# A four-layer vision tower on one core: zero matmuls in TensorE's waits, norms by ACT's root, and a rebuilt last layer

## The reference

```
h = patches @ W.T + b
layer 0: gated attention (relu(q k / 1024 + bias)^2, u * (kernel @ v) @ Wo); 8 experts of 256 hidden, top 1, capacity, relu
layer 1: complex linear recurrence over the 36 tokens of an image;           8 experts of 64 hidden, top 2, gelu
layer 2: scores = max over d of (Q + K), causal, top 8 of 36, softmax, @ V;  8 experts of 128 hidden, top 2, gelu, own norm inside
layer 3: attention softmax(h W h.T / 8) h;                                   H = gelu(h W1 + b1), 256 wide; 8 experts, top 1:
         out = probs[e] * (H @ Wd[e] + bd[e])
```

## Time and profile before

| what | us |
|---|---|
| median of 3 runs (225.05 to 229.84) | 228.05 |
| the profiled execution | 227.43 |
| its span, first to last instruction | 225.6 |
| busy in it: PE, DVE, ACT, POOL | 154.4, 106.0, 54.9, 35.2 |
| mean granted TensorE clock | 0.71 of 2.4 GHz |

### The profile page before, as it was taken

How to read it: one execution, slowest core, us unless ns; L and a number is a source line. 1 busy time by engine, 2 the same in 40 slices (tenths; PEclk the granted TensorE clock), 3 DMA queues, 4 the chain that set the end, 5 groups by cost and what they waited for, 6 DMA issues and landing times.

```text
span 225.6 us, 2568 instructions
## 1 busy us (share of the span) xinstructions
PE 154.4 (68%) x972; PEld 86.0 (38%) x972; DVE 106.0 (47%) x318; ACT 54.9 (24%) x89; POOL 35.2 (16%) x79
## 2 busy tenths in 40 slices
PE   0977289789996467896829301659996836999820
PEld 0435174544432324533513001446533425684220
DVE  2013762445566172652658996127372131024952
ACT  5302900155560000250100004204530250500100
POOL 7125000227760202002000000040002002000010
PEclk9995855589999555587666955575898575556975
DMA  6999100000000000000220000000000000000001
GB/s 194 407 292 375 64 3 0 0 3 1 1 0 3 0 0 0 0 1 0 32 49 1 0 0 0 3 0 0 3 0 1 0 3 0 0 0 0 0 0 26
DMA packets 4908, 8.25 MB, mean 37 GB/s; under 512 B 2744, under 2 KB 2872, under 8 KB 4768
## 3 DMA queue, kind: packets, MB, share of 16 engines
q1 hardware_dynamic: 4896, 8.10, 11.1%
HBM read 7.73 MB, written 0.37 MB: 36 GB/s over the span
## 4 chain that ended last, share of the span: by engine, by line
PE 50%; DVE 20%; issue 15%; POOL 5%; ACT 4%; DMA 4%; POOLq 1%; DVEq 0%
PE ps L400 11%; PE ps L413 7%; POOL rstd L284 5%; PE ps L371 4%; PE ps L364 3%; PE ps L407 3%; PE ps L465 3%; DVE scores L1090 3%; PE ps L382 2%; DVE hidden_gated L926 2%; PE ps L502 2%; DVE scores_rest L1101 2%; DMA weights_sb<-weights 1%; DMA k_parts_img<-k_scratch 1%; ACT squares L715 1%
## 5 line engine op out<-in xcount | busy, mean ns | idle before, releaser
L284 POOL TENSOR_TENSOR rstd<-var_eps,minus_half 96x6 f32<-96x6 f32 (+1 forms) x8 | 11.6, 1446 | 125.1 <-DVE var_eps L869 125.1
L926 DVE TENSOR_TENSOR hidden_gated<-hidden,ps 128x288 f32<-128x288 f32 x56 | 22.2, 449 | 13.3 <-PE ps L407 13.2
L727 ACT ACTIVATE hidden<-ps,weights_sb 128x576 f32<-128x576 f32 x28 | 20.6, 740 | 31.0 <-PE ps L400 30.9
L413 PE MATMUL ps<-hidden_gated,weights_sb 128*64 128x288 f32 x112 | 19.8, 432 | 0.6 <-DVE hidden_gated L926 0.5
L371 PE MATMUL ps<-consts_sb,rstd 96*64 96x96 f32 x108 | 10.8, 376 | 12.6 <-POOL rstd L284 12.6
L400 PE MATMUL ps<-h,weights_sb 64*128 64x288 f32 x80 | 18.1, 547 | 1.6 <-DVE h L874 1.3
L864 DVE COPY centred<-ps 128x288 f32<-128x288 f32 x8 | 3.7, 457 | 26.5 <-ACT squares L715 26.5
L715 ACT ACTIVATE squares<-ps 128x288 f32<-128x288 f32 x8 | 3.3, 410 | 44.9 <-PE ps L544 13.1
L371 PEld LDWEIGHTS ps<-consts_sb,rstd 96*64 96x64 f32 x108 | 8.4, 223 | 13.3 <-POOL rstd L284 13.3
L687 PE MATMUL ps<-weights_sb,hidden 128*128 128x512 f32 (+1 forms) x20 | 12.0, 766 | 0.0
L400 PEld LDWEIGHTS ps<-h,weights_sb 64*128 64x128 f32 x80 | 8.6, 235 | 9.1 <-ACT hidden L727 4.2
(11 more groups left out here) (247 smaller groups left out, 241.6 us busy)
## 6 DMA issues: line engine op xcount, KB each, us to landing
patch_sb<-patches SPq DMA_DIRECT2D x6, 288.0 KB, 5.7
weights_sb<-weights SPq DMA_DIRECT2D x1, 1108.0 KB, 9.7
weights_sb<-weights SPq DMA_DIRECT2D x1, 749.0 KB, 15.7
weights_sb<-weights SPq DMA_DIRECT2D x1, 689.0 KB, 14.3
weights_sb<-weights SPq DMA_DIRECT2D x1, 640.0 KB, 12.9
weights_sb<-weights SPq DMA_DIRECT2D x1, 512.0 KB, 11.4
weights_sb<-weights SPq DMA_DIRECT2D x1, 394.0 KB, 13.5
weights_sb<-weights SPq DMA_DIRECT2D x1, 375.5 KB, 6.8
```

What stands on the lines that cost most here:

```text
L284: pool.tensor_tensor(RS[:, 0:n], VE[:, 0:n], mhalf[0:TT, 0:n], ALU.pow).then_inc(S["rs"], 1)
L413: last = mm(PS[rows(h), YB, 0:HALF], w2[:, ch, :], HG[:, ch % GRING, h, :], start=False, stop=(ch == chunks - 1), skip_group_check=True)
L727: act.activation(HR[:, at % RING, :, :], two(ZA if ch % 2 == 0 else ZB), func, bias=w(f"b1_{n}")[:, ch:ch + 1]).then_inc(S["act_out"], 1)
L926: dve.tensor_tensor(HG[:, at % GRING, h, :], HR[:, at % RING, h, :], PS[:, G + h, 0:HALF], ALU.mult)\
```

## The change

- **Zeros.** `idle(n, bank)` issues n matmuls of 128x512 bf16 on an operand of zeros into a bank that is free then. 153 of them stand ahead of PE's waits: six at the start; two before each variance; one or three before and two after each spread; and in the attentions, the recurrence, the guard, the softmax and layer 3's attention (groups of 1 to 10). DVE clears the operand first, and five other tiles and one of ones, 5312 elements per partition, before anything else; selectors, gates and bias rows get 128 rows instead of 48 or 1 with zeros below. The two bias matmuls of V go ahead of the patches.
- **Norms.** After its squares ACT takes the root of the variances (`Sqrt` from PSUM), DVE the reciprocal; POOL's power is gone. `table(Sqrt)` is added before each squares but one, and the table of the next function follows the root: 16 calls of `table` instead of 8.
- **Experts.** Layer 0: the gates of a pair of chunks once for both, two downs, two ups. All layers: one DVE product of 576 columns per chunk. In layers 1 and 2 the gates of later chunks go to ZA and ZB too (`GATE_AT`).
- **Attention 0.** Residual and bias row go ahead of the scores and the kernel; half of the centring of the later weights moves behind the context's product. The load of those weights goes ahead of that of layer 0's experts.
- **Attention 2.** K is made from the centred rows before the norm is spread and scaled by the root's reciprocal on DVE. POOL subtracts the maximum and scales by the sum, taken from the eight top values, beside DVE's replacements; one DVE pass then selects. The router of layer 2 takes its logits from the centred rows with weights times gamma; its bias is made ahead.
- **Layer 3's experts.** The last router's logits come transposed: `Wg` as the 8-column stationary operand, then two matmuls to turn them. The bias is added by a bf16 matmul in three parts. Weights and bias are centred, so the last norm needs no mean; ACT squares with a sum, roots, and scales four of five tiles; stores go out tile by tile.

```diff

...
-            sp.dma_start(SL[:, :], sels).then_inc(S["sels"], 16)
+            sp.wait_ge(S["rows_zero"], 3)
+            sp.dma_start(SL[0:6 * E, :], sels).then_inc(S["sels"], 16)
...
+            sp.wait_ge(S["zero3"], 3)
+            sp.dma_start(BR[0:65:32, :], bias3).then_inc(S["bias3"], 16)
...
-                pool.wait_ge(S["ve"], k + 1)
-                n = 4 * NT if k == 5 else 2 * NT
-                pool.tensor_tensor(RS[:, 0:n], VE[:, 0:n], mhalf[0:TT, 0:n], ALU.pow).then_inc(S["rs"], 1)
...
+            pool.wait_ge(S["w_r2"], 16)
+            pool.tensor_scalar(WRG[:, :], w("Wr"), w("gam2"), None, ALU.mult).then_inc(S["wr_gam"], 1)
+            cut = ((0, 3), (3, QT))
+            pool.wait_ge(S["topped"], QT * HEADS)
+            for a, b in cut:
+                pool.tensor_tensor(SE[:, a:b, :, :].rearrange("p j h s -> p (j h) s"),
+                                   SC[:, a:b, :, :].rearrange("p j h s -> p (j h) s"),
+                                   top[:, a:b, :, 0].rearrange("p j h -> p (j h)").unsqueeze(2)
+                                   .to_broadcast([P, (b - a) * HEADS, SPAD]), ALU.subtract).then_inc(S["sub2"], 1)
+            pool.wait_ge(S["top_sum"], 1)
+            for n, (a, b) in enumerate(cut):
+                pool.wait_ge(S["exp2_out"], n + 1)
+                pool.tensor_tensor(SE[:, a:b, :, :].rearrange("p j h s -> p (j h) s"),
+                                   SE[:, a:b, :, :].rearrange("p j h s -> p (j h) s"),
+                                   d20[1][:, a * HEADS:b * HEADS].unsqueeze(2).to_broadcast([P, (b - a) * HEADS, SPAD]),
+                                   ALU.mult).then_inc(S["norm2"], 1)
...
+            def idle(n, bank):
+                for _ in range(n):
+                    mm(PS[:, bank, :], idle_in[:, 0:P], idle_in[:, :], start=True, stop=True)
...

+                bank = MB if k == 4 else ZA
...
                 pe.wait_ge(S["rs"], k + 1)
                 broadcast(psBC, 0)
+                idle(2, bank)

...
-                            .then_inc(S["gates"], 1)
+                        last = mm(PS[:, bank + h, 0:HALF], sel[:, g, h, :], CT3[:, :], start=True, stop=True)
+                    last.then_inc(S["gates"], 1)

...
+                    for pair in range(E):
+                        gate(pair, G, 2 * pair - 1 if pair > 0 else None)
+                        if pair == 0:
+                            bias2(True)
+                        else:
+                            down(2 * pair - 2)
+                            down(2 * pair - 1)
+                        for ch in (2 * pair + 6, 2 * pair + 7):
+                            if ch < chunks:
+                                up(ch)
+                    down(chunks - 2)
+                    down(chunks - 1)
...
+                        down(ch)
+                else:
+                    gate(0, G)
+                    up(7)
+                    gate(1, G, 0)
+                    pe.wait_ge(S["act_out"], BASE[2] + 7)
+                    gate(2, ZA)
+                    bias2(True)
+                    pe.wait_ge(S["act_out"], BASE[2] + 8)
+                    gate(3, ZB)
+                    gate(4, G, 1)
+                    down(0)
...
+            pe.wait_ge(S["filled"], 3)
+            pe.wait_ge(S["tok_w"], 16)
+            for j in range(2):
+                mm(PS[:, ZB + j, :].rearrange("p (a e) -> p a e", a=4), ones[:, 0:P],
+                   w("bv_row").unsqueeze(1).to_broadcast([P, 4, P]), start=True, stop=False, skip_group_check=True)
             pe.wait_ge(S["rows_c"], 2)
...
+            idle(8, G)
             pe.wait_ge(S["q_ready"], 1)
+            idle(4, G)
...
+            pe.wait_ge(S["wo_c"], 1)
+            mm(psY, w("bo_row"), ones[:, :], start=False, stop=False, skip_group_check=True)
+            idle(2, G)
...
+            for t in range(NT):
+                last = mm(PS[0:TT, ZA, t * P:(t + 1) * P], XC[:, cols(t)], w("wk"), start=True, stop=True)
+            last.then_inc(S["k_done"], 1)
...
+            idle(8, ZA + 1)
+            pe.wait_ge(S["wr_bet"], 1)
             pe.wait_ge(S["q_parts"], 3)
+            idle(10, MB)
...
                     n += 1
+            pe.wait_ge(S["score_red"], n)
+            idle(7, MB)
+            pe.wait_ge(S["topped"], QT * HEADS)
+            idle(7, MB)
+            pe.wait_ge(S["top_sum"], 1)
+            idle(7, MB)
+            pe.wait_ge(S["replaced"], QT * HEADS)
+            idle(4, MB)
...
+            pe.wait_ge(S["wr_gam"], 1)
+            pe.wait_ge(S["xc"], 6)
+            logits(2, XC, WRG[:, :])
+            idle(1, ZA)
             pe.wait_ge(S["rs"], 6)
...
+                return HH[:, ch, 4 * P:TOK] if q == 0 else HH[:, ch, (q - 1) * P:q * P]
+            def y3(q):
...
+                mm(PS[32 * h:32 * h + 32, YB, 0:D], HP[:, 2 * P:HALF], c("ident")[:, rows(h)], start=True, stop=True)
+            for q in range(1, FT):
+                last = mm(PS[:, YB, q * D:(q + 1) * D], HP[:, ((q - 1) % 2) * P:((q - 1) % 2 + 1) * P],
+                          c("ident")[:, rows((q - 1) // 2)], start=True, stop=True)
...
+            def bias(q):
+                mm(y3(q), one3[:, 0:n3(q)], BD3[:, :], start=True, stop=False, skip_group_check=True)
+            def part(q, ch):
...
+            def logits_T(ch):
+                for q in range(1, FT):
+                    mm(PS[32 * (q - 1):32 * (q - 1) + E, MB, 0:P], w("Wg")[:, ch * E:(ch + 1) * E], tok3(q, ch),
+                       start=False, stop=(ch == 1), skip_group_check=True)
+                return mm(PS[0:E, MB, P:P + 64], w("Wg")[:, ch * E:(ch + 1) * E], tok3(0, ch),
+                          start=False, stop=(ch == 1), skip_group_check=True)
...
-                for ch in range(2):
-                    last = mm(PS[0:n3(i), MB, i * E:(i + 1) * E], tok3(i, ch), w("Wg")[:, ch * E:(ch + 1) * E],
-                              start=(ch == 0), stop=(ch == 1))
...
+            part(0, 0)
+            pe.wait_ge(S["logits3_in"], 1)
...
+            for q in range(1, FT):
+                bias(q)
+                part(q, 0)
+                part(q, 1).then_inc(S["y3_done"], 1)
...
+                act.wait_ge(S["var"], k + 1)
+                if k == 5:
+                    act.activation(SD[0:TT, 2 * NT:4 * NT], psVar, ACT.Sqrt, bias=eps[0:TT, 1:2], scale=1.0 + EPS)\
+                       .then_inc(S["sd"], 1)
+                act.activation(SD[0:TT, 0:2 * NT], psVar, ACT.Sqrt, bias=eps[0:TT, 0:1]).then_inc(S["sd"], 1)
...
+                act.wait_ge(S["tile3"], q + 1)
+                act.activation(R2[0:p, q, :], R[0:p, q, :], ACT.Square, accum_out=ss[0:p, q:q + 1]).then_inc(S["ss"], 1)
...
-                if k == 5:
-                    step(dve.tensor_scalar(VE[:, 2 * NT:4 * NT], psVar, 1.0 + EPS, EPS * EPS, ALU.mult, ALU.add))
-                    sync()
-                dve.tensor_scalar(VE[:, 0:2 * NT], psVar, EPS, None, ALU.add).then_inc(S["ve"], 1)
...
+            dve.memset(idle_in[:, :], 0.0).then_inc(S["still"], 1)
+            dve.memset(SL[:, :], 0.0).then_inc(S["rows_zero"], 1)
+            dve.memset(CT3[:, :], 0.0).then_inc(S["rows_zero"], 1)
+            dve.memset(CTF[:, :], 0.0).then_inc(S["rows_zero"], 1)
+            dve.memset(BD3[:, :], 0.0).then_inc(S["zero3"], 1)
+            dve.memset(one3[:, :], 1.0).then_inc(S["zero3"], 1)
+            dve.memset(BR[:, :], 0.0).then_inc(S["zero3"], 1)
...
                 return x.rearrange("p (h t e) -> p h t e", h=2, t=NT)

-            dve.tensor_copy(by_half(kp3[:, 0, :]), psK).then_inc(S["k_parts"], 1)
...
+            te20 = TE[:, :, :, :].rearrange("p j h s -> p (j h) s")
...
+                    link(dve.tensor_reduce(d20[0][:, :], te20, AX, ALU.add))
+                    dve.reciprocal(d20[1][:, :], d20[0][:, :]).then_inc(S["top_sum"], 1)
                 for h in range(HEADS):
-                    step(dve.match_replace(REP[:, j, h, :], top[:, j, h, :], SC[:, j, h, :], 3 * NEG))
...
+                        .then_inc(S["replaced"], 1)
+            dve.wait_ge(S["replaced"], QT * HEADS)
+            dve.wait_ge(S["norm2"], 2)
+            dve.scalar_tensor_tensor(PR[:, :, :, 0:SPAD].rearrange("p j h s -> p (j h) s"),
...
+                dve.wait_ge(S["y3_done"], q + 1)
+                step(dve.tensor_tensor(YM[0:p, q, :, 0:E],
+                                       PS[0:p, 4 if q == 0 else q - 1, :].rearrange("p (d e) -> p d e", e=E),
+                                       comb[0:p, q, :].unsqueeze(1).to_broadcast([p, D, E]), ALU.mult))
...
+                dve.wait_ge(S["hres_in"], 1 if q == 0 else 2)
+                sync()
+                dve.tensor_reduce(R[0:p, q, :], YM[0:p, q, :, :], AX, ALU.add).then_inc(S["tile3"], 1)
```

449 lines of the change are left out of this document (262 added, 187 removed).

## The result

The changed kernel takes **169.44 us** (median of 4, 169.17 to 169.58) against 226.91 (4 runs, 225.05 to 229.84) of the kernel before on the same chip: ratio 0.749, 95% interval 0.744 to 0.754. The forecast was 179.5 with a range from 167 to 198, so the kernel gained 57.5 us where 47.8 were forecast (from 227.43, the profiled execution). Its profiled execution took 169.38, with a span of 167.5.

What follows compares the result with a forecast made beforehand. The kernel was taken as one dependent chain, bound by link lengths and TensorE's low clock. Ten stage savings sum to 58.7 us; less 3, 5 and 2.9, 47.8 off 227.43 gives 179.6, stated as 179.5, range 167 to 198.

Steps and rivals of the forecast that it cites:

- the deduction of 10.9: Whole kernel: allowance taken off the summed stage savings of 58.7 us, leaving 47.8 us saved.
- everything hides: Rival for the whole kernel: no loss at all, 169 us; chance 0.08.
- The clock's share: Stages 1 to 10: 26 us of the summed saving come from TensorE held at 2.4 GHz.
- 1.1 for the root against the power: Each norm: ACT's root and DVE's reciprocal, 0.55 us, replace 1.66 us around POOL's power; 1.1 us saved.
- the cover of 2.1: Behind each norm's root: reciprocal, spread, product and next matmuls, some 2.1 us, hide the table switch.
- the rival at 191: Norms: the eight added table switches aren't covered and add 11.8 us to 179.5; chance 0.12.
- Stage 1: 0 to 14.71 us, patches and bias of V: 3.2 us saved (2.3 to 4.3), DVE's memsets hidden.
- Stage 3: 37.64 to 73.67 us, norm 1, experts 0 and guard: 5.4 us saved (3 to 8).
- Stage 5: 92.27 to 116.78 us, experts 1, K and Q: 4.1 us saved, K's two transfers unchanged.
- Stage 6: 116.78 to 139.94 us, scores, selection, softmax: 4.8 us saved, 3.8 of it by softmax passes beside replacements.
- Stage 8: 153.51 to 170.96 us, experts 2: eight DVE products of 0.76 set the pace; 3.9 us saved (2.5 to 5).
- Stage 10: 192.55 to 225.60 us, last experts and head: 12.9 us saved (9 to 15), DVE's router starting some 4.3 earlier.

Runs made afterwards that it cites:

- fewer_zeros: Changed kernel with one zero matmul fewer at each of three places per norm (single ones ahead of the spread stay): 168.77, 173.35, 169.20 and 173.11 us.
- no_zeros: Changed kernel with none of the 153 zero matmuls, all else kept: 192.58 us, ratio to the kernel before 0.852.
- pool_power: Changed kernel with the reciprocal root of all eight norms taken by GpSimd's power again: 184.05 us.
- dve_softmax: Changed kernel with the softmax passes of the selection back on VectorE behind the replacements, one exponential on ScalarE: 174.71 us.
- plain_router: Changed kernel with the last router in its old form, 20 products of 8 columns behind 128x128 weight loads: 171.88 us.
- double_zeros: Changed kernel with each group of zero matmuls twice as long: 187.71 us, ratio to the kernel before 0.830.
- two_products: Changed kernel with each of VectorE's 28 expert products of 128x576 cut into two of 128x288: 170.28 us.

## Why the prediction was right, and where not

**What bounds it, and the direction.** Right. The clock and the length of each link were the two levers, and both gave what the stages said: 58.1 of 58.7.

**The step that failed: the deduction of 10.9.** It read "3 for zeros that outlast their waits, 5 for stretches where the clock falls all the same, 2.9 for handovers and terms I have rounded well". The first was mis-sized: the two shorter executions of `fewer_zeros` gained only 0.2 to 0.7, and the timeline has the zeros end inside their waits or up to 0.2 late. The second didn't occur: the windows show 0.90 in the selection and 1.00 or 0.98 everywhere else. The one low stretch (0.50 from 102.15 to 104.30) lies beside VectorE's maxima, where PE had only zeros to do. The third wasn't there, since the rounding went both ways. The rival "everything hides", 169 us, which I gave 0.08, is what happened within half a microsecond. It was the sum itself, and it should have been the forecast: I had worked out bounds for each term and taken a middle value, and then charged for the same doubts a second time.

**The clock's share.** Forecast 26 of the 58.7, measured 23.1 by `no_zeros`, or some 24 to 25 with the same transfer of K. The rest, forecast 32.7, measured 34. But the split is softer than I wrote it: `pool_power`, `dve_softmax` and `plain_router` lost up to 5, 0.9 and some 1.6 us of clock besides their own length. A shorter wait is also one that the same zeros fill.

**Norms.** 1.1 for the root against the power: measured 1.08. The two instructions and their handovers, taken at 0.55, measured about 0.6 (from the end of the variance at 60.04 to the spread's first load at 60.64). The root of 96x6 takes 0.26 and the reciprocal 0.19.

**Tables.** Costing them at nothing was right; the cover of 2.1 was too small by a third: in norm 0 it is 3.0. I left out that ScalarE's first work waits for the first group of matmuls to end. With that the rival at 191 would have got less than 0.12.

**Stage 1.** 3.4 for 3.2, with the unknown at its dear end. The timeline of the kernel after has DVE's memsets:

```profile
0.84 0.27 DVE L1093 MEMSET idle_operand<- 128x256 uint32 x1 [0.84 <-PEq L1543]
1.39 1.34 DVE L1094 MEMSET selectors<- 128x1536 uint32 x1 [0.27 <-issue]
...
4.06 0.49 DVE L1022 TENSOR_REDUCE row_sums<-weights_sb 128x6 f32<-128x384 f32 x1
```

1536 elements of uint32 take 1.34 us and 256 take 0.27: 0.84 ns for each further element. I had taken 3.2 us for 5312, 0.60 each. The memsets are hidden all the same: most of the bf16 zeros are written as uint32, two to an element, so that the seven shapes add up to 3120 elements and not to the 5312 that I had counted, and VectorE is through when the weights land, at 4.1. Rate and count were both wrong and cancelled, by luck; the end of the stage is 11.28 for a forecast of 11.5. The Trainium skill (VectorE: DVE Perf Modes, "Zero memsets can be issued as uint32 (trn2)") says both that zeros in bf16 can be issued as uint32, half as many elements, and that an element takes one cycle whatever the type. The trace agrees with the first, and with the type making no difference (512 elements of f32 take 0.48, 128 of bf16 0.17); how long a cycle is it doesn't say, but an element of these memsets takes less time than one of VectorE's products (128x576 in 0.751 and 128x288 in 0.449, 1.05 ns each). I had used the second half of the section and missed the first.

**Stage 3** gave 4.6 for 5.4, inside its 3 to 8. **Stage 5** gave 3.7 for 4.1: SyncE waited 3.5 us for the write of K's parts where it waited 1.6 before, and TensorE then 0.84 for the transfer behind it. I had held the two transfers fixed; with them fixed the stage would have given 0.84 more. Over the runs this wait was 1.6 in the kernel before, in `no_zeros` and in `double_zeros`, and between 3.0 and 3.6 in the kernel after and the ten others; what sorts them was not tried and stays open.

**Stage 6** gave 6.3 for 4.8. From the last maximum to the transposes I forecast 5.7; it is 5.3. GpSimd does 480 columns of a shift in 1.15 us and 320 in 0.73, 2.3 to 2.4 ns a column, near the dear end of my 1.5 to 2.5, and its second pair is through before the last replacement (108.29 against 108.50). Ahead of the maxima the stage saved 1.7 (11.1 before, from 116.78 to 127.92, and 9.46 after, from 92.69 to 102.15), where I had 1.0.

**Stage 8** gave 2.2 for 3.9. The step was "from its end eight DVE products of 0.76 set the pace". They don't; TensorE's 7.5 us of gates and downs do, as the chain above shows, and `two_products` fits it by costing no more than 0.8. I had priced what VectorE would need, and hadn't added up TensorE's work for the same chunks.

**Stage 10** gave 13.5 for 12.9. That the transposed router would bring the logits some 4.3 earlier was wrong as a cause: VectorE takes them 3.3 earlier in the stage (8.63 us behind its start before, 5.38 after), but at the high clock the old form gives them no later. What counts there is when the output matmuls start and at which clock, which I hadn't separated.

## What to carry to other kernels

When every stage is costed by its own rows with bounds, don't subtract a general allowance for the same doubts at the end; keep them in the range. In a latency-bound kernel on TensorE (one whose time is a chain of dependent steps) fill each wait with zeros up to just short of its length, and shorten the waits: each of the two made the other worth more here (zeros 17.5 in the old kernel and 23.1 in the new; the rest 34 without zeros and 39.6 with them). Measure several executions with fewer zeros before choosing their number: with 21 of 153 left out, two of four executions were 4 us longer. Before naming the engine that sets the pace of a group, add up the work of every engine for that group at the clock it will have.

## What the runs showed of the hardware that was not expected

- A table load behind a table load costs 1.28 + 0.20 each, with no gap that a drain would fill (2.98 us from the first load's start to ScalarE's next real work).
- TensorE's clock fell though PE showed as busy throughout: behind 20 matmuls of 8 columns with wide weight loads (`plain_router`) the granted clock of the next 3.5 us was 0.57. It was 1.00 in the same window of the kernel after, where loads of 8 columns with 128 or 64 streamed columns each take their place.
- A reduction on VectorE over strided columns is dearer than over contiguous ones. In the kernel after 1024 strided columns (L1326) took 2.00 us and the tail's sum of 576 contiguous ones (L1376) 0.75, 1.3 ns a column instead of 2. The same sum in the kernel before, 512 columns read with a stride (L1169), took 1.03: the new layout saves 0.28 per tile while it also takes in the residual.
